# Spread casts, a last block with four banks and 54 opening identity products in a two-layer transformer kernel

## The reference

```
layer 0:  h = rms(x) * (w * (1 + cond @ tw.T));  q, k, v = h @ Wq.T, h @ Wk.T, h @ Wv.T   (8 heads of 64, one k and v)
          x = x + softmax(rope(q) rope(k).T / 8) v @ Wo.T
          h = rms(x) * ...;  x = x + (silu(h @ Wg.T) * (h @ Wu.T)) @ Wd.T
layer 1:  h = ln(x) * (scale1 + 1) + shift1;  16 heads of 32, q and k normalised
          x = x + attention(h) @ Wproj.T * gamma1
          u = (ln(x) * (scale2 + 1) + shift2) @ Wfc1.T + bfc1
          x = x + (0.5 * u * (1 + tanh(c * (u + 0.044715 u^3))) @ Wfc2.T + bfc2) * gamma2
```

## Time and profile before

| | us |
|---|---|
| median of 3 runs | 2583.48 |
| lowest, highest | 2580.83, 2583.75 |
| profiled execution, its time | 2578.21 |
| profiled execution, its span | 2576.3 |
| PE busy in the span | 2504.8 (97%) |
| DVE, POOL, ACT busy | 1387.2, 1065.0, 962.0 |

### The profile page before, as it was taken

The page is one execution under the profiler, slowest core; times in us unless marked ns, Lnnn a source line. Parts: engine busy times, 40 slices in busy tenths (PEclk is TensorE's granted clock), DMA queues, the critical chain, the costliest instruction groups (busy, mean ns, idle before and its releaser), DMA issues.

```text
span 2576.3 us, 47329 instructions
## 1 busy us (share of the span) xinstructions
PE 2504.8 (97%) x18448; PEld 1259.4 (49%) x18448; DVE 1387.2 (54%) x2150; ACT 962.0 (37%) x1560; POOL 1065.0 (41%) x1007
## 2 busy tenths in 40 slices
PE   6799999999999999999999999999999999999998
PEld 5445444454444544445454445554545455454543
DVE  7574343443434434344586575766757585766741
ACT  4452232322323223232343452626445362635442
POOL 3342222322223223222354455656556564665532
PEclk8999999999999999999999999999999999999999
DMA  6520101001010010100422312021211302121110
GB/s 221 172 68 17 39 3 51 5 17 39 3 53 3 18 39 3 53 3 15 135 71 84 124 31 79 26 63 41 56 59 30 88 28 73 34 59 43 48 43 29
DMA packets 113109, 133.21 MB, mean 52 GB/s; under 512 B 44686, under 2 KB 56078, under 8 KB 112916
## 3 DMA queue, kind: packets, MB, share of 16 engines
q1 hardware_dynamic: 112916, 130.26, 16.6%
HBM read 75.83 MB, written 18.74 MB: 37 GB/s over the span
## 4 chain that ended last, share of the span: by engine, by line
PE 84%; DVE 4%; POOL 4%; issue 3%; ACT 3%; DMA 1%; SPq 0%; POOLq 0%; DVEq 0%; ACTq 0%
PE ps_m L1572 46%; PE ps_abef L1572 18%; PE ps_d L1572 2%; PE ps_c L1572 2%; PE ps_abef L1772 2%; PE ps_abef L1779 2%; PE ps_abef L1774 2%; PE ps_abef L1808 1%; PE ps_d L1758 1%; PE ps_c L1624 1%; POOL inner L921 1%; POOL scratch L949 1%; PE ps_abef L1816 1%; PE ps_abef L1797 1%; POOL scratch L953 1%
## 5 line engine op out<-in xcount | busy, mean ns | idle before, releaser
L1572 PE MATMUL ps_m<-h_mlp,weights 128*128 128x512 f16 x3264 | 749.9, 381 | 16.6 <-ACT scratch L1185 10.0
L1572 PE MATMUL ps_m<-weights,inner 128*128 128x512 f16 x3072 | 695.2, 380 | 2.1 <-DVE scratch L1405 2.1
L1572 PEld LDWEIGHTS ps_m<-h_mlp,weights 128*128 128x128 f16 x3264 | 313.4, 98 | 380.4 <-ACT scratch L1185 16.2
L921 POOL TENSOR_TENSOR inner<-scratch,inner 128x512 f16<-128x512 f32 x256 | 312.1, 1219 | 400.4 <-ACT inner L1106 400.3
L1572 PEld LDWEIGHTS ps_m<-weights,inner 128*128 128x128 f16 x3072 | 296.4, 98 | 336.7 <-issue 5.3
L1572 PE MATMUL ps_abef<-h_mlp,weights 128*128 128x512 f16 x1344 | 310.9, 379 | 0.0
L1106 ACT CAST inner<-scratch 128x512 f16<-128x512 f32 x256 | 157.0, 613 | 155.4 <-DVE scratch L1405 84.7
L1572 PEld LDWEIGHTS ps_abef<-h_mlp,weights 128*128 128x128 f16 x1344 | 127.2, 98 | 144.8 <-issue 4.2
L899 POOL TENSOR_TENSOR h_mlp<-scratch,h_mlp 128x512 f16<-128x512 f32 x64 | 74.0, 1156 | 191.3 <-ACT h_mlp L1061 191.3
L961 POOL TENSOR_TENSOR scratch<-scratch 128x512 f32<-128x512 f32 x64 | 72.6, 1134 | 159.0 <-DVE scratch L1459 159.0
L1061 ACT CAST h_mlp<-scratch 128x512 f16<-128x512 f32 x64 | 39.5, 618 | 262.4 <-POOL scratch L961 142.0
(11 more groups left out here) (170 smaller groups left out, 3667.7 us busy)
## 6 DMA issues: line engine op xcount, KB each, us to landing
x_mlp<-x_attn SPq DMA_DIRECT2D x64, 256.0 KB, 2.3
scratch<-scratch SPq DMA_DIRECT2D x128, 128.0 KB
weights<-gamma SPq DMA_DIRECT2D x128, 128.0 KB, 2.9
x_attn<-x SPq DMA_DIRECT2D x32, 256.0 KB, 2.6
x_mid<-x_mlp SPq DMA_DIRECT2D x32, 256.0 KB, 2.0
x_attn<-x_mid SPq DMA_DIRECT2D x32, 256.0 KB, 2.7
out<-x_mlp SPq DMA_DIRECT2D x32, 256.0 KB, 2.2
inner<-wada_t SPq DMA_DIRECT2D x4, 1024.0 KB, 8.4
```

What stands on the lines that cost most here:

```text
L921: nc.gpsimd.tensor_tensor(inner[:, 1, j, :], src[:, j % 2, :], inner[:, 0, j, :], ALU.subtract).then_inc(L.m_lo, 1)
L1572: ins = nc.tensor.matmul(o, left(a, k), right(b, k), start=(first and n == 0), stop=(last and n == len(order) - 1), skip_group_check=True)
```

## The change

There are four parts.

1. **Casts spread.** In `START1` the two halves of a `cut` of the fc2 strips become two steps with times of their own: `cut` is now ACT's half, `cut_lo` DVE's. The loads of the strips move too: all four stand ahead of the first spread of v on SP.
2. **Last block with four banks.** Block 7 of layer 1 has its own list `LAST1` with other lags, and its strips go round over four banks (`ways(False)` is 4) and four working buffers. The second pair of banks and the second pairs of buffers were the attention's, which has no work left then; the first use of each waits once for the attention's last step.
3. **Identity products.** Before its first set of products PE multiplies the float16 identity by itself 54 times, 128 columns each, into `ps_d`, which nothing reads before it is written again.
4. `mlp_lo` and `mlp_hi` take the buffer as an argument; the instructions are the same.

```diff
 SETUP_START1 = [
-    (3.2, "load1", "fc2_0"), (14.7, "cut", "fc2_0"), (19.8, "cut", "fc2_1"), (31.3, "load1", "fc2_1"),
-    (36.6, "load1", "fc2_2"), (37.2, "cut", "fc2_2"), (37.2, "cut", "fc2_3"), (58.0, "load1", "fc2_3")]
+    (3.0, "load1", "fc2_0"), (3.4, "load1", "fc2_1"), (12.5, "cut", "fc2_0"), (17.7, "cut_lo", "fc2_0"),
...
+LAGS1_LAST = {"up": [("u", -0.1), ("arg", 1.3), ("tanh", 3.0), ("gelu", 3.8), ("m_hi", 5.4), ("m_lo", 6.0)],
+              "down": LAGS1["down"]}
+LAST1 = with_mlp([], JOBS1, LAGS1_LAST, PE_COST)
...
+        u1_parts = [u1[:, n] for n in range(2)] + [qkt_words[:, 512 * n:512 * (n + 1)] for n in range(2)]
+        g1_parts = [g1[:, n] for n in range(2)] + [p1_words[:, 512 * n:512 * (n + 1)] for n in range(2)]
...
+        def ways(attention_beside):
+
+            return 2 if attention_beside else 4
...
                     if stage == "u":
                         act.wait_ge(L1.up, it * IC + j + 1)
-                        act.wait_ge(L1.m_lo, it * IC + (j - 1 if j > 1 else 0))
+                        w = ways(both)
+                        act.wait_ge(L1.m_lo, it * IC + max(j + 1 - w, 0))
...
+                        if not both and j == 2:
+                            act.wait_ge(L1.scores, NBLK * TILES)
+                            act.wait_ge(L1.p_turned, NBLK * TILES)
-                        nc.scalar.activation(u1[:, j % 2, :], ps_m[j % 2][:], ACT.Identity, bias=b_fc1_t[:, j:j + 1],
+                        nc.scalar.activation(u1_parts[j % w], ps_m[j % w][:], ACT.Identity, bias=b_fc1_t[:, j:j + 1],
...
-                if piece == "cut":
+                if piece == "cut_lo" or (piece == "cut" and not which.startswith("fc2")):
                     cut_lo(no_of(which))
...
             pe.wait_ge(s_const, 39)
+            for n in range(54):
+                nc.tensor.matmul(ps_d[:, 0:P], ident16[:], ident16[:], start=True, stop=True)
...
-                            if j >= 2:
-                                pe.wait_ge(L1.u, it * IC + j - 1)
+                            if j >= ways(both):
+                                pe.wait_ge(L1.u, it * IC + j + 1 - ways(both))
+                            elif j >= 2:
+                                pe.wait_ge(L1.masked, NBLK * TILES)
+                                pe.wait_ge(L1.pt, NBLK * TILES)
+                                pe.wait_ge(L1.pt2, NBLK * TILES)
...
-            block1(NBLK - 1, STEADY1, False)
+            block1(NBLK - 1, LAST1, False)
```

More of the change, by code:

```diff
@@ L198 @@
                                                      for n in range(4)])
-SETUP_STEPS = ("consts", "rows", "bias", "load", "load1", "cut", "cut1", "ada", "ada_out", "ang", "sin", "rope", "rope_out")
+SETUP_STEPS = ("consts", "rows", "bias", "load", "load1", "cut", "cut1", "cut_lo", "ada", "ada_out", "ang", "sin", "rope", "rope_out")
 MLP0 = SETUP_STEPS + ("gate", "up", "down", "gamma_m", "tanh", "gated", "m32", "m_hi", "m_lo", "y", "store")
@@ L975, in _ @@
                 if stage == "m_lo":
-                    mlp_lo(L0, act0, NBLK - 1, a)
+                    mlp_lo(L0, act0[:, a % 2, :], NBLK - 1, a)
             def block1(it, both):
-                for stage, j in STEADY1:
+                for stage, j in (STEADY1 if both else LAST1):
                     if both and stage not in MLP1:
@@ L982, in block1 @@
                     if stage == "m_lo":
-                        mlp_lo(L1, u1, it, j)
+                        mlp_lo(L1, u1_parts[j % ways(both)], it, j)
                     if stage == "y":
@@ L1189, in block1 @@
                             act.wait_ge(L1.y, tile(it, 0))
-                        nc.scalar.activation(g1[:, j % 2, :], u1[:, j % 2, :], ACT.Square,
+                        nc.scalar.activation(g1_parts[j % w], u1_parts[j % w], ACT.Square,
                                              scale=(0.044715 * GELU_C) ** 0.5).then_inc(L1.usq, 1)
@@ L1193, in block1 @@
                         act.wait_ge(L1.arg, it * IC + j + 1)
-                        nc.scalar.activation(g1[:, j % 2, :], g1[:, j % 2, :], ACT.Tanh).then_inc(L1.act, 1)
+                        g = g1_parts[j % ways(both)]
+                        nc.scalar.activation(g, g, ACT.Tanh).then_inc(L1.act, 1)
                     if stage == "m_hi":
-                        mlp_hi(L1, u1, it, j)
+                        mlp_hi(L1, u1_parts[j % ways(both)], it, j)
             block1(0, START1, True)
@@ L1886, in block1 @@
             def block1(it, both):
-                for stage, job in STEADY1:
+                for stage, job in (STEADY1 if both else LAST1):
                     if both and stage not in MLP1:
```

27 lines of the change are left out of this document (14 added, 13 removed), and 2 rows, old and new, of the table SETUP_START1.

## The result

The changed kernel took 2565.18 us in the median of 4 runs (2564.36 to 2566.6), the kernel before 2582.15 (2579.49 to 2583.75): ratio 0.9937, interval 0.9921 to 0.9953. 2570.5 us had been predicted, from 2563.5 to 2577. The profiled execution took 2565.41 us (span 2563.5), where 2578.21 (2576.3) stood before: 12.8 us between the profiles for 13.0 predicted.

A forecast was written before the change was run, and what follows sets the result against it. PE was taken as the bound, busy 2504.8 of 2576.3 us, so only its idle time, half clock or work could matter. 10.5 + 2.2 + 0.3 = 13.0 us off the 2583.48 median gave 2570.5, range 2563.5 to 2577.

The forecast's parts named there:

- Last block, 10.5 us: Last block: four banks and new step order let PE run through; gain 10.5 us, bounds 8.0 and 11.6.
- Rival C: Last block: ACT sets the pace at 2.75 us a strip instead of 2.3; 2573.0 us in all; chance 9%.
- First block of layer 1, 2.2 us: First block of layer 1: spread casts gain 0.0 + 2.0 + 0.2 = 2.2 us, bounds -2.5 and 8.
- The first stop: First block of layer 1: PE's 3.10 us stall before 1464.37 moves to another place as about 3.3; gain 0.0.
- the ring: First block of layer 1: chain from `u` to difference; third cut holds it, `u` of strip 6 at 1471.95, today 1471.93.
- The second stop: First block of layer 1: PE's 4.29 us stall before 1494.70 shrinks with one low half less; gain 2.0 us.
- The clock: First block of layer 1: less half-clock time on PE; 0.2 us taken, may give back or cost 2.5.
- Opening, 0.3 us: Opening: 54 identity products lift the clock, saving 3.3 us on PE's first set but 0.3 on the path.
- rival D: Opening: identity products do not lift the clock, only 0.3 us missing; 2570.8 us in all; chance 4%.
- Rival A: First block of layer 1: casts free of the ring, later stall shrinks, 6 us instead of 2.2; 2566.7 us; chance 20%.
- B: First block of layer 1: casts give nothing, block costs 1.5 us instead; 2574.2 us in all; chance 15%.
- E: Opening up to 120 us: clock changes shift, half clock meets its work; no faster, or 2589 us; chance 2%.

The follow-up runs named there:

- late_cut: Whole change with the first layer-1 block's third cut later and the softmax parts ahead of strip 8's, POOL keeping its old order; gain in the block 0.3 us.
- second profile of before: The kernel before, unchanged, profiled once more: 2577.97 us, where its first profiled execution took 2578.21.
- late_cut_2: Whole change with both last low halves behind the softmax in the first layer-1 block and POOL on the new list; block 3.0 us better than in the whole change.

## Why the prediction was right, step by step

- **Last block, 10.5 us: 10.55 in eight kernels.** The surplus left at the bias was 1.0 predicted, and PE waits 0.87, with 0.17 for the last product to come out. Rival C (ACT sets the pace) is refuted: `u` waits 0.20 us for PE at each strip. Not separated in the prediction: the banks are 10.02 of it, the order 0.53.
- **First block of layer 1, 2.2 us: 1.96, term by term.** The first stop was to be worth 0.0, since PE would stand at strip 6 where it stands now. So it came. The first of the strips' products in this stretch and the one with which strip 6 begins, before:

```profile
1455.28 5.99 PE L1572 MATMUL ps_m<-h_mlp,weights 128*128 128x512 f16 x27
...
1472.67 1.47 PE L1572 MATMUL ps_m<-h_mlp,weights 128*128 128x512 f16 x6 [0.30 <-ACT scratch L1185]
```

  and the same two products with the change:

```profile
1451.40 8.58 PE L1588 MATMUL ps_m<-h_mlp,weights 128*128 128x512 f16 x39
...
1468.70 2.49 PE L1588 MATMUL ps_m<-h_mlp,weights 128*128 128x512 f16 x6 [3.56 <-ACT scratch L1200]
```

  The change is 3.88 us ahead at the first and 3.97 at the second: a gain of 0.09. In between it was up to 3.26 us further ahead, and the ring took that back. The stop behind the third cut was predicted at about 3.3 us and is 3.56; late_cut, which put that cut behind the steps in question, removed it. The second stop fell from 4.29 to 2.53, 1.8 us for 2.0. The clock was to give 0.2. Half clock from 1469.0 costs 1.2 us, less a small wait of before that went (0.41, counted in); half clock behind the second stop lasts 3.4 us instead of 6.8 and gives back 1.1. With 0.2 us in small pieces between, this is the whole: 0.09 - 1.22 + 0.21 + 1.76 + 1.12 = 1.96. Sums of idle time mislead here: up to the second of the products above PE's stops sum to 3.40 us before (3.10, 0.30) and 5.03 now (1.47, 3.56), and yet nothing was lost, for the most part because before's half-clock stretch from 1465.7 lay where PE would otherwise have waited; the second profile of before shows this. One statement was wrong: that PE would not stop at 1461.3. The turn behind the norms stops it 1.47 us, since its DVE step (L1449) stands behind the second low half; the ring, which binds later, hides this. The size of the clock term was luck in part: with the same casts and the same stops the block gave 0.43 to 3.97 us, inside the 2.5 either way that the bounds had.
- **The inversions.** A low half of 2.29 us (1452.17) lies inside an inversion of 2.92 (1451.67), both at their usual length, as rows 9 and 10 had it. The rule of the Trainium skill (SBUF — State Buffer, Who interferes with whom) that whoever starts first holds the pair (the memory ports that DVE and POOL share) is borne out for the differences (2.75 us behind the third low half) and not for a low half that starts inside an inversion. The trace agrees with it for several long ones in a row too: in late_cut_2 the two low halves take 3.25 and 4.21 us instead of 2.29 each, and the low part of P 3.99 instead of 2.12. The first low half waits until POOL's difference ends at 1479.66, the low part of P (from 1479.80) until this low half ends at 1481.80, and the second low half until the low part of P ends at 1483.79; with these waits taken off, each has its usual length within 0.2 us.
- **Opening, 0.3 us: 0.07 in the profile, and not to be told from its spread.** The first set took 3.79 us (3.73 predicted) and rival D is refuted. The Trainium skill's rule (TensorE: Matmul & The Clock Gate, Part 1) that activity lifts the default low clock agrees: PE has run identity products since 3.33 us when the granted clock rises to 1.00 at 8.1 us. It falls again at 14.9, while PE waits for DVE, and the 3.3 us won on PE meet DVE's queue as said.
- **Not in the sum at all:** the gaps at the returns, -2.5 us in layer 0 and +3.7 in layer 1, and the half-clock stretch gone from the crossing, -1.67. They cancel to -0.5, and 0.3 us were lost in small pieces elsewhere. That 13.0 met 12.8 so closely is therefore luck in part: these terms, up to 3.7 us each, were missing and happened to cancel, as did the clock's in the first block. That the code's place would matter was no rival of mine.
- Rival A (the stall behind the third cut shrinks) and B (the casts give nothing) did not come; nor did E. The median came out at 2565.18, 5.3 us below the 2570.5 predicted. The step that failed there is the one from profile to median: the prediction took the distance of before's profiled execution from its median (5.3 us) to be the same after the change, and there the profiled execution lay 0.2 us above the median. The range held.

## What to carry to other kernels

When a stall is removed by moving work, follow the moved work to the next consumer on the same engine: the third cut's stop came back at the scores, then at the tenth strip, then at the products with V, where DVE had no idle time left. Judge what a stop costs by the shift of the same product in two profiles and not by its idle time: a wait and a half-clock stretch can stand in for each other. Products that are free by themselves are not free by their place: compare the gaps at loop returns before and after any change of an instruction count, and try a few counts. Compare two profiles stretch by stretch at the same product; totals of 13 us hid a spread of 5 us in the first 125 us.

## What the runs showed of the hardware that was not expected

- Time from product to product at a loop's return: 0.21 to 1.35 us, and it changes with the number of PE instructions ahead of the loop. 256 added changed the sums of five returns by 0.1 and 0.7 us, 108 added gave 2.5 us less in one layer and 3.7 more in the other. The instruction transfers in the trace of the kernel before are 16,384 bytes each (166 of them on q8).
- The same stop can be followed by half clock or not. The one of 2.12 us in the crossing is in all 14 profiles; before, nine products after it took 3.47 us, with the change 2.10:

```profile
1386.64 3.47 PE L1572 MATMUL ps_m<-weights,inner 128*128 128x512 f16 x9 [2.12 <-DVE scratch L1405]
```

```profile
1384.44 2.10 PE L1588 MATMUL ps_m<-weights,inner 128*128 128x512 f16 x9 [2.12 <-DVE scratch L1421]
```

  It was so in the seven profiles with 54 or 65 products ahead, and in none of the seven with 0 or 128, whatever the shift at that point (from -2.5 to +4.7 us). Why is open.
